# Masks of all attention heads added into the bias tiles by accumulating DMAs

## The reference, cut to what matters

```python
q = (x @ Wq + bq).reshape(B, S, N_HEAD, HEAD_DIM).transpose(0, 2, 1, 3)   # k, v alike
scores = jnp.einsum('bhqd,bhkd->bhqk', q / math.sqrt(HEAD_DIM), k)
scores = scores + attention_bias              # (8, 16, 512, 512) float32
scores = jnp.where(src_mask, -jnp.inf, scores.astype(jnp.float32))   # (8, 1, 512, 512)
probs = jax.nn.softmax(scores, axis=-1).astype(v.dtype)
ctx = jnp.einsum('bhqk,bhkd->bhqd', probs, v)
```

## Time and profile before

| | |
|---|---|
| median of 3 runs | 2626.97 us (2624.86 to 2627.95) |
| profiled execution, its own time | 2626.6 us |
| its span | 2624.8 us |
| TensorE busy | 2509.0 us, 96% |
| VectorE | 2019.1 us, 77% |
| ScalarE | 1147.3 us, 44% |
| GpSimd | 1136.5 us, 43% |
| granted TensorE clock, mean | 0.985 |

### The profile page before, as it was taken

How to read it: one execution, slowest core, us unless ns; L and a number is a source line. 1 busy time by engine, 2 the same in 40 slices (tenths; PEclk the granted TensorE clock), 3 DMA queues, 4 the chain that set the end, 5 groups by cost and what they waited for, 6 DMA issues and landing times.

```text
span 2624.8 us, 47276 instructions
## 1 busy us (share of the span) xinstructions
PE 2509.0 (96%) x14583; PEld 1242.2 (47%) x14583; DVE 2019.1 (77%) x3863; ACT 1147.3 (44%) x2189; POOL 1136.5 (43%) x951
## 2 busy tenths in 40 slices
PE   6999999999999999779999999999999999999996
PEld 4455555555555555434444444444444444444443
DVE  7877777777777777778878688679687786886787
ACT  3666666666676767533322223223223222232231
POOL 1464646464646464434344143343342441532430
PEclk8999999999999999989999999999999999999998
DMA  6444445454544545352322232132223222322240
GB/s 209 142 155 155 159 147 163 146 166 147 163 146 158 154 151 161 126 180 92 112 90 85 82 121 89 59 124 89 92 90 101 97 77 82 126 92 78 97 152 33
DMA packets 155507, 320.56 MB, mean 122 GB/s; under 512 B 17474, under 2 KB 23234, under 8 KB 155218
## 3 DMA queue, kind: packets, MB, share of 16 engines
q1 hardware_dynamic: 145426, 299.13, 34.9%
q10 hardware_dynamic: 9792, 17.83, 1.9%
HBM read 298.85 MB, written 17.86 MB: 121 GB/s over the span
## 4 chain that ended last, share of the span: by engine, by line
PE 42%; issue 7%; POOL 4%; DVE 4%; ACT 1%; DVEq 0%; POOLq 0%; ACTq 0%; DMA 0%
PE ffn_bank L1382 13%; PE ffn_bank L1384 13%; PE ffn_bank L1383 13%; PE ffn_bank L1368 2%; POOL x L1319 1%; POOL stage L1305 1%; POOL f L1295 1%; PE ffn_bank L1448 1%; PE ffn_bank L1389 1%; ACT g L1523 0%; DVE g2T_hi L1697 0%; DVE g2T_lo L1698 0%; DVE stage L1607 0%; DVE f L1725 0%; DVE stage L1641 0%
## 5 line engine op out<-in xcount | busy, mean ns | idle before, releaser
L1000 DVE CUSTOM_DVE_ANT_0 tiles<-bank,stage 128x512 f32<-128x512 f32 x512 | 323.9, 686 | 79.5 <-PE bank L628 74.7
L792 ACT ACTIVATE tiles<-tiles,nmax 128x512 f32<-128x512 f32 x512 | 363.5, 713 | 44.6 <-DVE nmax L1000 44.5
L508 POOL TENSOR_TENSOR stage<-stage,mask_add 128x1024 f32<-128x1024 f32 x128 | 272.1, 2137 | 202.3 <-DMA stage<-in_bias 183.0
L651 PE MATMUL bank<-ident,tiles 128*128 128x128 f32 x2048 | 300.2, 280 | 15.7 <-ACT pT L778 4.3
L1697 DVE CAST g2T_hi<-g 128x512 f16<-128x512 f32 x256 | 193.9, 757 | 154.5 <-ACT g L1523 149.0
L651 PEld LDWEIGHTS bank<-ident,tiles 128*128 128x128 f32 x2048 | 222.7, 140 | 175.5 <-issue 83.2
L1698 DVE TENSOR_TENSOR g2T_lo<-g,g2T_hi 128x512 f16<-128x512 f32 x256 | 272.1, 1063 | 8.8
L1523 ACT ACTIVATE g<-ffn_bank,bi 128x512 f32<-128x512 f32 x128 | 87.9, 687 | 361.0 <-PE ffn_bank L1384 316.5
L1382 PE MATMUL ffn_bank<-w_hi,g2T_hi 128*128 128x512 f16 x512 | 197.5, 386 | 35.1 <-DVE g2T_lo L1698 35.1
L1312 POOL TENSOR_TENSOR stage<-grid,f 128x512 f32<-128x512 f32 x64 | 104.8, 1657 | 268.1 <-DVE stage L1633 144.3
L778 ACT ACTIVATE pT<-bank 128x512 f32<-128x512 f32 x256 | 150.9, 589 | 150.4 <-PE bank L651 150.4
(11 more groups left out here) (291 smaller groups left out, 5142.4 us busy)
## 6 DMA issues: line engine op xcount, KB each, us to landing
stage<-in_bias SPq DMA_DIRECT2D x256, 512.0 KB, 4.2
stage<-in_W_l SPq DMA_DIRECT2D x128, 512.0 KB, 3.3
grid<-in_grids SPq DMA_DIRECT2D x160, 256.0 KB, 3.5
xin<-in_x SPq DMA_DIRECT2D x36, 256.0 KB, 4.0
out<-stage ACTq DMA_DIRECT2D x36, 256.0 KB, 2.0
x_rows<-tiles ACTq DMA_DIRECT2D x32, 256.0 KB, 3.0
stage<-in_W SPq DMA_DIRECT2D x16, 512.0 KB, 4.8
x2n<-x_rows SPq DMA_DIRECT2D x8, 1024.0 KB, 7.0
```

The source lines that it names most:

```text
L508: pool.tensor_tensor(bias[:, n % NB, :, :], bias[:, n % NB, :, :], mask_add[:, u % T, :].unsqueeze(1).to_broadcast([P, 2, S]), ALU.add).th ...
L651: mm = pe.transpose(bank[:, t * P:(t + 1) * P], tiles[:, 4 * (u % NR) + i, t * P:(t + 1) * P], ident[:, :])
L792: act.activation(tile, tile, ACT.Exp, scale=-1.0, bias=nmax[:, u % 2, i:i + 1], accum_out=rsum[:, j, h:h + 1]).then_inc(prob_ready, 1)
L1000: dve.tensor_tensor_reduce(tiles[:, 4 * (u % NR) + i, :], bank[:, :], bias[:, half % NB, i % 2, :], -1.0, 3.0e38, ALU.add, ALU.min, nmax[: ...
```

## The change

GpSimd no longer adds the mask with its arithmetic, and TensorE no longer opens banks 2 and 3 with a mask product. Instead, GpSimd issues one accumulating DMA for each of the 32 bias tiles of a pass: once the tile's load has landed, the DMA adds the bf16 mask block, repeated for the two heads, to the float32 tile. VectorE waits for that DMA's semaphore ahead of heads 0 and 2. TensorE's score products all start their banks themselves, and each claims its bank just before it. The wait of TensorE for the mask is gone.

```diff
--- before.py
+++ after.py
@@ -286,7 +286,7 @@
         ctx_split = sem("ctx_split")
         x2_ready = sem("x2_ready")
         x2_out = sem("x2_out")
-        masked = sem("bias_masked")
+        mask_summed = [sem(f"mask{i}_summed") for i in range(NB)]
         chain = sem("dve_chain")
         carrier = sem("wait_carrier")
         sp_carrier = sem("sp_wait_carrier")
@@ -503,10 +503,11 @@
                     pool.tensor_tensor(x1[:, t, :], xin[:, t, :], bo[:, :], ALU.add).then_inc(x1b_ready, 1)
                 pool.wait_ge(mask_ready, it * 1 + 1)
                 for u in range(NQ):
-                    n = 2 * u
-                    pool.wait_ge(bias_in[n % NB], (it * USES[n % NB] + n // NB + 1) * 16)
-                    pool.tensor_tensor(bias[:, n % NB, :, :], bias[:, n % NB, :, :],
-                                       mask_add[:, u % T, :].unsqueeze(1).to_broadcast([P, 2, S]), ALU.add).then_inc(masked, 1)
+                    for n in (2 * u, 2 * u + 1):
+                        pool.wait_ge(bias_in[n % NB], (it * USES[n % NB] + n // NB + 1) * 16)
+                        pool.sem_inc(pool_carrier, 1)
+                        pool.dma_start(bias[:, n % NB, :, :], mask_add[:, u % T, :].unsqueeze(1).to_broadcast([P, 2, S]),
+                                       accum_op=ALU.add).then_inc(mask_summed[n % NB], 16)
                     for part in POOL_L0.get(u, ()):
                         if part[0] == "up_bias":
                             up_bias(it)
@@ -614,19 +615,14 @@
 
                 def scores(u):
                     g, j = u // T, u % T
-                    if u == 0:
-                        pe.wait_ge(mask_ready, it * 1 + 1)
                     if j == 0:
                         pe.wait_ge(q32_ready, it * C + g + 1)
                         pe.wait_ge(k32_ready, it * C + g + 1)
                     for i in range(4):
-                        bank = claim(pe, it, ("S", u, i))
-                        if i >= 2:
-                            pe.matmul(bank[:, :], ident_bf[:, :], mask_add[:, j, :], start=True, stop=False)
-                    for i in range(4):
                         rows = slice(HD * i, HD * i + HD)
+                        claim(pe, it, ("S", u, i))
                         pe.matmul(psum[i][:, :], q32[rows, g, j * P:(j + 1) * P], k32[rows, g, :],
-                                  start=i < 2, stop=True).then_inc(full[i], 1)
+                                  start=True, stop=True).then_inc(full[i], 1)
 
                 def values(v, kb):
                     g = v // 2
@@ -992,10 +988,8 @@
                         if i < 4 and u < NQ:
                             half = n // 2
                             bank = arrived(dve, it, ("S", u, i))
-                            if i == 0:
-                                dve.wait_ge(masked, it * NQ + u + 1)
-                            if i == 2:
-                                dve.wait_ge(bias_in[half % NB], (it * USES[half % NB] + half // NB + 1) * 16)
+                            if i in (0, 2):
+                                dve.wait_ge(mask_summed[half % NB], (it * USES[half % NB] + half // NB + 1) * 16)
                             dve.sem_inc(carrier, 1)
                             dve.tensor_tensor_reduce(tiles[:, 4 * (u % NR) + i, :], bank[:, :], bias[:, half % NB, i % 2, :],
                                                      -1.0, 3.0e38, ALU.add, ALU.min, nmax[:, u % 2, i:i + 1])\
```

## The result

The changed kernel takes 2717.19 us (median of four runs, 2710.16 to 2721.89) against 2627.46 us before: 1.0343 times the time, with a 95% interval of 1.0321 to 1.0364, so some 90 us slower. The forecast was 2755 us in a range of 2570 to 2960.

What follows compares the result with a forecast made beforehand. TensorE was taken to bound the kernel before, the DMA engines after: 17.9 us more per pass, 143 us in eight, less 15 for running ahead, gave +128 us, 2755 us, in a range of 2570 to 2960.

Steps and rivals of the forecast that it cites:

- The bound before: In the loop of eight sequences TensorE sets the pace, busy 128.0 of 130 us; everything else has room on average.
- Price of one accumulating DMA: Time of all 16 DMA engines per bias tile: 2.45 us, as 1.5 loads by bytes read; bounds 1.63 to 3.26.
- The first rival: Two whole reads or dearer: 3.26 us of the engines per accumulating DMA, 2962 us in all; chance 0.18.
- The stretch: Mask cast's end to last slot's first score: 26 loads plus 32 accumulating DMAs take 120.8 us, 17.9 longer per pass.
- The 15 us taken off for running ahead during the opening: Over the kernel, 15 us caught in each pass's opening 7.7 us, before any refill is due.
- The mask products give nothing back: TensorE's 256 dropped products, 66.6 us in all, yield no gain because arrivals set the stretch.
- GpSimd's issues: On GpSimd's queue, 32 issues per pass at 0.53 to 2.14 us each fit the 103 us stretch; nothing added.
- the third rival: GpSimd becomes the bound from 2.5 us per issue; at 3 us, 2747 us in all; chance 0.10.
- Latency: Refill of the six-tile ring: 8 us left for a transfer taking 4.2 to 6 us; costed at nothing unless transfers queue.
- The rival of a faster kernel: Transfers of at most 1.63 to 1.7 us fit, TensorE's 50 us come through: 2577 us; chance 0.32.
- The signs: In the loop: DMA share near 0.9, later loads, VectorE waiting 18 us per pass, TensorE down 60 us, passes about 146 us.
- the lower clock: TensorE at its lower clock level would push the time towards the range's upper end; no size given.

Runs made afterwards that it cites:

- e7: Kernel before with only GpSimd's additions (heads 0 and 1) given to accumulating DMAs, TensorE's products kept for heads 2 and 3: 2629.60 us, ratio 1.0016.
- e1: Separate kernel that only moves 512 KB tiles, each transfer kind eight times; engine time each: bf16 accumulation 2.50 us, float32 2.78, copy within the chip 1.35, load 1.48.
- e3: Changed kernel with TensorE's mask products of heads 2 and 3 put back: 2717.41 us, ratio 1.0350.
- e6: Changed kernel, but from slot 6 on tile 2u + 1 is masked by GpSimd's addition; 22 DMAs and 10 additions per pass: 2669.82 us, ratio 1.0165.
- e12: Accumulating DMAs for both tiles without products in slots 9 to 15, the kernel before's scheme in slots 0 to 8; 14 DMAs per pass: 2677.74 us, ratio 1.0202.
- e8: Changed kernel with the two rstd chains of a pass moved from GpSimd to VectorE, all 32 accumulating DMAs kept: 2693.37 us, ratio 1.0255.
- e11: Accumulating DMAs for both tiles without products in slots 1 to 8, the kernel before's scheme in the other slots; 16 DMAs per pass: 2614.20 us, ratio 0.9956.
- e4: Changed kernel with half of its accumulating DMAs: tile 2u by GpSimd's addition, tile 2u + 1 by DMA, no products: 2693.54 us, ratio 1.0265.
- e9: Kernel before with only the rstd chains moved from GpSimd to VectorE, as a control: 2680.33 us, ratio 1.0202.

## Why the prediction was right, and where not

*The bound before* was right: TensorE, with GpSimd and the loads in time. e7 changed only GpSimd's part and moved the time by 4 us.

*Price of one accumulating DMA.* 2.45 us was forecast, 2.37 measured in the kernel, 2.50 alone. The reason given, bytes read in units of a load, was only near the truth: e1 shows close to two copies within the chip. The first rival's law was thus the better one, but its unit, the load from memory, was too dear; 2 x 1.35 = 2.7 would have been its price. That 2.45 came so near 2.37 is in part luck.

*The stretch.* 120.8 us were forecast, 109.9 to 115.1 measured. The transfer of the pass's last tile lands behind slot 15's first score (in the pass shown at 464.92 against 462.80), so 31 stand in the stretch: with 2.37 the sum is 42.4 + 73.5 = 115.9 us, against 112.7 on average. The rest is the overlap of packets (115.9 / 112.7 = 1.03, the DMA share of the stretch). The 15 us taken off for running ahead during the opening have no measured source: the stretch of 102.9 us already held the opening. Small terms were not foreseen: 1.7 us per pass after the last score, and a first score that came 0.5 us later, when six transfers start at once beside the loads of x, ada and mask. Two larger ones were not foreseen either, and they work against each other: the overlap, by this sum some 26 us in eight passes, and GpSimd's chains, at least 24 us. That the total came within 38 us of the forecast owes something to this.

*"The mask products give nothing back"* was right in sum (e3), not slot by slot: slots 1 to 7 do get shorter. The sum over a stretch hid that the room is uneven. The step that failed here is the cover by averages: room for 32 transfers was counted over 102.9 us, where the short slots 8 to 14 have 5.5 us each against 8.0 needed. It did not change the sign, because the whole was over-full too. In e6 and e12, where the whole was not, the same reasoning forecast at most 2620 and 2625 us; measured were 2670 and 2678.

*GpSimd's issues.* Between 0.53 and 2.14 us were given, 1.20 us measured (median), where SP's in the earlier trace rows were 0.53; the third rival's price of 2.5 us did not occur. But what stands between the issues was costed at nothing as long as GpSimd's total fits. e6's timeline and e8's 24 us show that a chain of 6 us ahead of an issue is felt.

*Latency* was costed at nothing with 8 us of room. One transfer alone lands in 4.5 us; in the full queues it took 9.0 and its load 7.6, together 16.6 us, where three slots are 13.6 us in the plain places and up to some 25 us in slots 1 to 3. As forecast, the cover goes when transfers queue.

*The rival of a faster kernel* failed on its price, 1.7 us at most, not on its mechanism: where the slots are long, some of TensorE's time does come through, which is e11.

*The signs.* The DMA share (0.9 or above forecast, 1.03), the later loads (7.6 us against 4.2) and the waits at VectorE for mask DMAs (18 us per pass forecast, 19 measured, 5 of them in the opening) came as named. Passes were 141 us and not 146. TensorE's busy time did not fall by 60 us, it rose by 9. The forecast named the lower clock as a push towards the upper end and put no term for it into the sum; the clock was at the lower level for 79 us of the eight stretches.

## What to carry to other kernels

Price an accumulating DMA as about two copies of its destination's size within the chip (2.4 to 2.5 us against 1.35 here), put it beside the loads on the same 16 engines, and compare with the length of each slot that it must fit, not with the average of the stretch; the ring here holds three slots, and e12 shows that room further off did not help. When the busiest engine starts to wait, look at its granted clock as well: here the slot behind a wait ran at half of it. Before giving work to GpSimd's DMA queue, list what else stands on that queue: an issue behind a 6 us chain plus a landing of 5 to 9 us replaces an addition that was done in 2.1 us. A scheme that loses as a whole can win in the slots that have room: the mixed kernel e11, 16 accumulating DMAs per pass in slots 1 to 8, was the fastest of all.

## What was not expected of the hardware

Beside additions and DMA issues of GpSimd in an unbroken run a VectorE cast within the chip took 5.3 us and another operation 6.5 us, against 0.43 and 0.35 us with issues alone (e4). A single rstd chain of thirteen tiny operations cost 2.8 us of a slot on VectorE (e9), where GpSimd's 6.1 us had been free. And a bf16 source of half the bytes made an accumulating DMA only a tenth cheaper than a float32 source (2.50 and 2.78 us).
